# Node degrees added up tile by tile on VectorE and summed by one product, in a fused graph, mix and FFN block on one core

## What is computed

```python
xn = layernorm(x)
deg = segment_sum(ones, dst);  deg_inv = 1 / max(deg, 1)
layer(h) = h @ W_self + (segment_sum(h[src], dst) * deg_inv) @ W_neigh + b
gnn = layer1(relu(layer0(xn)))
mix = gelu(V @ Wo + bo)      # V from Q, K = elu(..)+1 of xn, one sum over all rows
x = x + gnn + mix
x = x + ffn(layernorm(x))    # FFN with 16-bit activation and 4-bit weight rounding
```

## Time and profile before

| | us |
|---|---|
| median of 3 runs (lowest, highest) | 1191.91 (1191.04, 1192.41) |
| the profiled execution, its own time | 1191.83 |
| its span in the trace | 1190.0 |
| PE busy | 1155.2 |
| DVE busy | 673.0 |
| ACT busy | 356.2 |
| POOL busy | 389.8 |

### The profile page before, as it was taken

How to read it: one execution, slowest core, us unless ns; L and a number is a source line. 1 busy time by engine, 2 the same in 40 slices (tenths; PEclk the granted TensorE clock), 3 DMA queues, 4 the chain that set the end, 5 groups by cost and what they waited for, 6 DMA issues and landing times.

```text
span 1190.0 us, 15232 instructions
## 1 busy us (share of the span) xinstructions
PE 1155.2 (97%) x6303; PEld 622.6 (52%) x6303; DVE 673.0 (57%) x1232; ACT 356.2 (30%) x446; POOL 389.8 (33%) x224
## 2 busy tenths in 40 slices
PE   4899999999999999999999999999999999999978
PEld 3555555555555554444444555444444445479934
DVE  7866846748475673344432634746563345582663
ACT  5635234243333323322311122313110012252540
POOL 1266675867768674677500000000000000000000
PEclk8999999999999999999999999999999999999989
DMA  9946436253442439533811135323220080000005
GB/s 260 340 90 155 106 50 154 20 137 61 95 111 19 94 72 320 127 54 88 310 49 40 61 118 180 109 73 110 85 89 18 18 159 1 1 1 1 2 13 160
DMA packets 156151, 117.61 MB, mean 99 GB/s; under 512 B 93401, under 2 KB 132569, under 8 KB 155058
## 3 DMA queue, kind: packets, MB, share of 16 engines
q1 hardware_dynamic: 86744, 103.41, 27.9%
q0 software_dynamic: 69024, 13.07, 8.5%
q10 hardware_dynamic: 314, 0.16, 0.0%
HBM read 90.13 MB, written 21.41 MB: 94 GB/s over the span
## 4 chain that ended last, share of the span: by engine, by line
PE 94%; DVE 4%; issue 1%; ACT 1%; DMA 0%; POOLq 0%; POOL 0%; ACTq 0%
PE ps L1057 34%; PE ps L987 32%; PE ps L1084 7%; PE ps L1118 7%; PE ps L1159 6%; PE ps L1189 3%; PE ps L974 2%; DVE stats L1205 1%; PE ps L1105 1%; DVE xnT L1259 0%; PE ps L995 0%; PE ps L951 0%; PE ps L944 0%; DMA x_all<-in_x_dram 0%; DVE ln L1214 0%
## 5 line engine op out<-in xcount | busy, mean ns | idle before, releaser
L598 POOL DMA_INDIRECT at_scratch<-copies,cell x160 | 342.2, 2139 | 166.7 <-DMA at_scratch<-copies,cell 100.4
L987 PE MATMUL ps<-xnT,whl 128*128 128x512 f16 (+1 forms) x2160 | 381.8, 339 | 0.0
L987 PEld LDWEIGHTS ps<-xnT,whl 128*128 128x128 f16 x2160 | 210.6, 98 | 168.9
L1057 PE MATMUL ps<-hb,hT 128*128 128x512 f16 x960 | 207.7, 379 | 1.3 <-DVE hT L1524 1.3
L1057 PEld LDWEIGHTS ps<-hb,hT 128*128 128x128 f16 x960 | 93.9, 98 | 114.5 <-DVE hT L1524 1.8
L1057 PE MATMUL ps<-hb,VT 128*128 128x512 f16 x480 | 103.9, 379 | 1.5 <-ACT S_b L740 1.5
L1057 PE MATMUL ps<-hb,xnT 128*128 128x512 f16 x480 | 104.2, 379 | 0.0
L579 POOL PARTITION_ALL_REDUCE ag_fw<-am_fw x9 | 3.2, 354 | 306.5 <-DVE am_fw L1407 306.5
L1084 PE MATMUL ps<-AT,P 125*128 125x512 f16 (+1 forms) x480 | 84.9, 339 | 0.0
L1118 PE MATMUL ps<-P,AT 125*128 125x512 f16 x360 | 79.0, 379 | 0.0
L1491 DVE SCALAR_TENSOR_TENSOR P<-ps,P 125x512 f16<-125x512 f32 x40 | 27.4, 688 | 88.9 <-ACT P L822 88.8
(11 more groups left out here) (231 smaller groups left out, 1211.7 us busy)
## 6 DMA issues: line engine op xcount, KB each, us to landing
raw<-in_L_gnn_W_neigh_dram SPq DMA_DIRECT2D x32, 512.0 KB, 4.6
raw<-in_L_gnn_W_self_dram SPq DMA_DIRECT2D x24, 512.0 KB, 5.3
key_b<-key_scratch SPq DMA_DIRECT2D x8, 1250.0 KB, 6.8
raw<-in_L_mix_Wo_dram SPq DMA_DIRECT2D x16, 512.0 KB, 3.7
parts<-at_scratch POOLq DMA_DIRECT2D x20, 312.5 KB, 4.6
at_scratch<-zeros POOLq DMA_DIRECT2D x6, 1020.0 KB, 17.8
x_all<-in_x_dram SPq DMA_DIRECT2D x9, 512.0 KB
x_acc<-in_x_dram SPq DMA_DIRECT2D x9, 512.0 KB
```

What stands on the lines that cost most here:

```text
L598: pool.indirect_dma_start(out=at_scr[c % 2][:, :], out_offset=bass.IndirectOffsetOnAxis(ap=cell[:, c:c + 1], axis=0), in_=copies[:, c:c + ...
L987: mm = pe.matmul(acc_of(c)[:, a:b], whl[:, i, wp, k, :], xnT[:, k, ap, a:b], start=(k == 0 and wp == 0 and ap == 0), stop=(k == KC - 1 and ...
L1057: mm = pe.matmul(half_bank(i), stationary[:, k, ap, t * TP:t * TP + P], hb[:, n % 2, k, wp, :], start=(k == 0 and wp == 0 and ap == 0), st ...
```

## The change

Seven edits, in the order of the execution:

1. POOL fills `zeros` ahead of `once`, and no longer behind `spare_c`.
2. DVE takes the statistics of tile 5 right behind `x_scale(1)`, ahead of `turned_lo(0)`; before, behind `turned_lo(1)`.
3. DVE adds the ten tiles of `AT` into `dinvb` (float32) with nine additions of 128 x 1250, three each behind tiles 33, 34 and 35 (`add_degrees`, `DEG_ADDS`).
4. `degrees` on PE is a product of a float32 matrix of ones with `dinvb`: two matmul calls of 512 columns behind tile 37 and one of 226 columns behind tile 38. The first waits for all nine additions. DVE's two copies of the result with max(deg, 1) come behind its tiles 37 and 38. The wait for the last of `AT` moves to the first aggregation product.
5. ACT does `turned_x2(7)` ahead of the last root instead of behind it.
6. The 6 matmuls of `keep_busy` ahead of `all_max` are gone; the 12 stay.
7. DVE's order of `code_lin` and `code_low` is another: `code_lin` 2 and 3 come behind `code_low(1)`.

```diff
-        DEG_TILE = 36
+        DEG_TILE = 37
+        DEG_ADDS = {33: (1, 2, 3), 34: (4, 5, 6), 35: (7, 8, 9)}
...
+            pool.memset(zeros[:, :], 0.0).then_inc(zeros_set, 1)
+
             steps(pool.memset(once[:, :], 1.0))
...
-            pool.memset(zeros[:, :], 0.0).then_inc(zeros_set, 1)
...
             for t in range(NT):
+                if t + 1 == NT:
+                    turned_x2(t - 2)
                 act.wait_ge(v2_ok, t + 1)
                 act.activation(ln[:TP, 1, t:t + 1], ln[:TP, 0, t:t + 1], ACT.Sqrt).then_inc(std2_ok, 1)
-                if t + 1 == NT:
-                    turned_x2(t - 2)
                 second_norm(t)
...
             def degrees(a, b):
-                for s in range(NT):
-                    for c in range(a, b, 512):
-                        d = min(c + 512, b)
-                        mm = pe.matmul(bank(6, 2)[:, c - a:d - a], ones16[:TP, :], AT[:TP, s, c:d],
-                                       start=(s == 0), stop=(s == NT - 1))
+                for c in range(a, b, 512):
+                    d = min(c + 512, b)
+                    mm = pe.matmul(bank(6, 2)[:, c - a:d - a], ones32[:TP, :], dinvb[:TP, c:d], start=True, stop=True)
                 mm.then_inc(deg_done, 1)
...
-                    if i == DEG_TILE - 1:
+                    if i == DEG_TILE:
                         pe.wait_ge(so_ok, WN1 + 1)
-                        pe.wait_ge(at_ok, NT + 1)
+                        pe.wait_ge(deg_added, NT - 1)
                         degrees(0, 1024)
                     elif i == DEG_TILE + 1:
                         pe.wait_ge(deg_free, 1)
...
             pe.wait_ge(w9_in[2 * IC], 16)
-            keep_busy(6, bank(5), w9(2 * IC, 0, slice(0, P)), w9(2 * IC, 0, slice(0, 512)))
             pe.wait_ge(all_max, X2 + 1)
             keep_busy(12, bank(5), w9(2 * IC, 0, slice(0, P)), w9(2 * IC, 0, slice(0, 512)))
...
             x_scale(1)
+            x_stats(5)
             turned_lo(0)
             prepare_scale(0)
             turned_lo(1)
-            x_stats(5)
             turned_lo(2)
...
+            def add_degrees(s):
+
+                if s == 1:
+                    dve.wait_ge(b1_ok, NT)
+                    dve.wait_ge(at_ok, NT - 1)
+                else:
+                    dve.wait_ge(deg_added, s - 1)
+                if s == NT - 1:
+                    dve.wait_ge(at_ok, NT)
+                dve.tensor_tensor(dinvb[:, :], AT[:, 0, 0:N] if s == 1 else dinvb[:, :], AT[:, s, 0:N],
+                                  ALU.add).then_inc(deg_added, 1)
...
                 if i in PART_TILE:
                     counts(PART_TILE[i])
+                for s in DEG_ADDS.get(i, ()):
+                    add_degrees(s)
                 if i == DEG_TILE:
-                    dve.wait_ge(b1_ok, NT)
                     degrees(0, 1024, 1)
-                elif i == DEG_TILE + 2:
+                elif i == DEG_TILE + 1:
                     degrees(1024, N, 2)
...
             code_lin(0)
             dve.tensor_scalar(s_ug[:, :], i_fw[:, :], sv[:, Q_X:Q_X + 1], None, ALU.mult).then_inc(s_ug_ok, 1)
-            for n in range(len(PIECES)):
-                if n + 1 < len(PIECES):
-                    code_lin(n + 1)
+            code_lin(1)
+            code_low(0)
+            for n in range(1, len(PIECES)):
                 code_low(n)
+                for later in ((2, 3) if n == 1 else (n + 2,)):
+                    if later < len(PIECES):
+                        code_lin(later)
```

More of the change, by code:

```diff
@@ L254, in build @@
         xs_ok, xt_done, xt_hi, xt_free = (sem(n) for n in ("xs_ok", "xt_done", "xt_hi", "xt_free"))
-        deg_done, deg_free, dinv_ok, dcol_done = (
-            sem(n) for n in ("deg_done", "deg_free", "dinv_ok", "dcol_done"))
+        deg_added, deg_done, deg_free, dinv_ok, dcol_done = (
+            sem(n) for n in ("deg_added", "deg_done", "deg_free", "dinv_ok", "dcol_done"))
         squares_ok, sums_ok, scale_ok, w_sums_ok = (
@@ L1076, in _ @@
                 par = (g + 1) % 2
+                if g == 0:
+                    pe.wait_ge(at_ok, NT + 1)
                 if g < 2:
```

## The result

The changed kernel takes 1187.70 us, median of 6 runs (1187.33 to 1188.38); the kernel before took 1191.97 us beside it on the same chip (6 runs, 1190.99 to 1192.41). The ratio is 0.9966, with a 95% interval of 0.9956 to 0.9976: faster by 4.3 us, inside the range 1185.4 to 1189.6, half a microsecond above the forecast. The profiled execution of after took 1187.40 us with a span of 1185.2 us, against 1191.83 and 1190.0.

A forecast was written before the change was run, and what follows sets the result against it. PE was taken as the bound, busy for 1155.2 of 1190.0 us. From 1191.83, minus 3.2 (degrees), minus 2.0 (second layernorm), plus 0.4 (start) gave 1187.1, stated as 1187.2 us for the median; range 1185.4 to 1189.6.

The forecast's parts named there:

- Degrees: PE's degree matmuls, 5.29 us, replaced by float32 calls of 2.1 us: gain 3.2 us (1.1 to 4.2), DVE's additions costing nothing.
- The margin of 1.7 us: Time between the ninth DVE addition's end at 641.1 and PE asking for it at 642.8, so PE would not wait.
- the three values weighed: Float32 degree product on PE: 1.1 us, 2.1 at the transposes' pace per column, or 4.2 at twice that pace; 2.1 taken.
- Second layernorm: Earlier `turned_x2(7)` and twelve fillers start the first up/gate product at 1053.6: gain 2.0 us (0.9 with all twelve slow).
- Start: Tile 5's statistics wait for their DMA and delay `turned_lo(0)` by 0.64 us: cost 0.4 us, range -0.2 to +1.9.
- The clock rival: The first up/gate product starts at the lower clock after PE's idle gaps, costing 1.9 us: 1189.0; chance 18%.
- The start's rival: The start loses more, through one more stretch at the lower clock or the DMA: around 1188.5; chance 8%.
- The dear product: PE's float32 degree product runs at twice the transposes' pace, 4.2 instead of 2.1 us: 1189.3; chance 7%.
- the held additions: DVE's additions take 2.53 us each, as beside POOL's own addition, and PE waits 7.7 us: 1194.8; chance 3%.
- the empty reordering: Reordering brings nothing at the second layernorm because PE's last transposes wait for something else: 1189.1; chance 2%.

The follow-up runs named there:

- the turn alone: Kernel before with only `turned_x2(7)` moved ahead of the last root, 18 fillers and the old coding order kept: 1191.23 us against 1191.99.
- the start alone: Kernel before with only `zeros` filled first and tile 5's statistics ahead of `turned_lo(0)`: 1191.81 us against 1191.99, ratio 1.0000.
- the order taken back: Changed kernel with the old loop order of `code_lin` and `code_low`: 1188.36 us against 1191.81 for the kernel before, ratio 0.9975.
- the float16 one: Changed kernel with the degree sums kept in a float16 tile and multiplied by float16 ones: 1185.71 us against 1191.81 for the kernel before.
- more additions: Changed kernel with three more DVE instructions on `dinvb` behind the ninth addition, PE waiting for all twelve: median 1190.95 us, one run of 6972.01 left out.
- the degrees alone: Kernel before with only the degrees' edits (additions on DVE, float32 product on PE, moved waits): 1189.14 us against 1191.99, ratio 0.9979.

## Why the prediction was right

**Degrees: as worked out.** The additions took 1.46 us each (1.43 to 1.46, forecast 1.49 with the wait), the ninth ended at 640.8 (forecast 641.1), and PE asked at 643.0 (forecast 642.8). The margin of 1.7 us was 2.2. The product, which no row of the trace showed, took 2.10 us: the transposes' pace per column held for wide ones. Of the three values weighed, 1.1, 2.1 and 4.2, the middle one was exact. The edit alone (1189.14) moved the chain by the same 3.19 us.

**Second layernorm: the size nearly right, the credit wrong and the size in part luck.** The first product starts 4.15 us behind the maximum, forecast 4.1, and the gain was 1.75, forecast 2.0. The quarter microsecond is largely the 0.16 us that a product pays behind an idle PE and doesn't behind a busy one; I took the start of before from a chain in which the fillers ran straight into it. Three readings were off. I counted the fillers as part of the path; the kernel with 18 of them is as fast as the one with 12, since at full clock 18 take 4.05 us and fit ahead of the coding. And I checked `code_low(1)` "now straight behind `code_low(0)`" only for being on time and gave the edit that puts it there no price. It has one: without it 0.8 us of the gain are lost, and the turn alone measured 0.76 us. And I took the 1055.62 of before, with its slow fillers, for the kernel's, where it is one execution's: the stretch that took 404.81 us there took 403.97 in the trace of the start alone, with the old code at this place. By the table above 0.84 of the gain is this, and 0.92 is the order of the coding, to which the sum gave nothing. Without the order, with the edits that the sum priced, the trace has 403.96: a gain of 0.85 where 2.0 was forecast. That the size came near is luck: the edit without a price supplied the other half.

**Start: right in sign, near in size.** The forecast was +0.4; the one trace gives +0.18, the means over the kernels' traces +0.3, and +0.1 without the two traces that have the lower clock under the first products. The transfer landed at 14.97, forecast 15.2. Taking only the statistics back gave 0.8 us, so the statistics in the hole cost more than the early fill of `zeros` gained. The fill's own part wasn't run alone against the kernel before; the first marks with it and with the statistics back (mean 62.09) against those with neither (62.61) put it at half a microsecond, an estimate from three and five traces. I had netted the two in one term, and so passed over that half of this edit was worth undoing.

**The clock rival did not come.** It was given 18%, since 2.62 us of idle time were followed by a granted clock of 0.5 before. In after three idle times of 1.19, 1.08 and 1.25 us were followed by 1.00, and under the first product no trace has the lower level. The length of the idle time alone doesn't decide it: in the trace of the start alone the same 2.62 us were followed by 1.00, and with the order taken back 1.19 and 1.06 us were followed by 0.50. The twelve fillers had been given 2.6, 3.6 or 5.2 us; they took 2.75 in after, 4.3 in the profiled executions of the kernel with the old coding order and of the float16 one, and 4.4 behind the old idle time of 2.62. In the first two of these the product still started within 0.3 us of its coding's end, where after has 0.14, so the spread cost at most 0.15 us. The start's rival, one more stretch at the lower clock there, did not come in after, but in two of the six traces with both start edits, and costs about 0.6 us. The dear product, the held additions and the empty reordering are out by the rows above.

**The rest.** The three terms measured 0.18 - 3.19 - 1.75, against 0.4 - 3.2 - 2.0: 0.04 apart in sum. The forecast sum is 1187.03, which I wrote as 1187.1. The profiled execution came to 1187.40 because of 0.37 us outside the span, for which the prediction had no term, and the median of the runs is 0.3 above that execution, where before it was 0.1. Runs of the kernels with the float32 product have 2.12 to 2.22 us outside the span (with more additions 1.90 to 2.19), those with the degrees of before 1.76 to 1.87, and those with the float16 sum 1.84 to 1.93 but for one run at 2.14. Its cause stays open, since nothing in a trace covers that time.

## What to carry to other kernels

An edit that lets an engine start earlier is worth only what the next piece it needs can follow: price the order of the pieces behind the first one as well as the first. Small whole numbers can be summed in float16 on VectorE and summed over partitions by one float16 product, at a quarter of the float32 product's time and a little over half of the additions'. Before work is moved into a hole on an engine, look up when its data lands: here it came 0.57 us too late, and the empty hole was the better one. And before a stretch with a low granted clock is priced as a gain, look at a second execution: here 0.84 us of it were there in some traces of the same code and not in others.

## What the hardware showed beyond the forecast

GpSimd's `affine_select` moved with the fill ahead of it. POOL's timeline of after:

```profile
1.25 3.50 POOL L569 MEMSET zeros<- 128x4080 f16 x1
4.68 0.20 POOL L571 MEMSET once<- 125x125 f32 x1
16.17 0.28 POOL L572 TENSOR_SCALAR_AFFINE_SELECT once<-once 125x125 f32<-125x125 f32 x1 [11.28 <-issue]
```

In the kernel with the degrees alone, where the fill stands behind it and the last `MEMSET` ahead of it ends at 1.45:

```profile
12.22 0.29 POOL L571 TENSOR_SCALAR_AFFINE_SELECT once<-once 125x125 f32<-125x125 f32 x1 [10.76 <-issue]
```

It follows 10.8 and 11.3 us behind the last `MEMSET` in these two, and 10.1 to 12.2 us in all 14 traces; the trace names no cause but issue. Where the fill of `zeros` stands behind it on POOL, it sets when the fill runs, and the fill held VectorE's `TENSOR_SCALAR` of three elements: in the five traces with the old place of the fill this instruction took 1.58 to 2.50 us and ended within 0.05 us of the fill's end, in the nine with the early fill it took 0.17 us. In the kernel before, the statistics (1.28 us), the reciprocal and a `TENSOR_SCALAR` of one element (0.15 us), which ran beside the same fill, kept their times.
